# A fused cross-attention and fp4 feed-forward kernel on one core: a split first load of the gate weights, and a new written order for the opening

## What is computed

```python
# attention over channels C = 256, in G = 8 groups of 32; inp_q = layernorm(x), inp_k = inp_v = ctx
t = Wt @ ctx;  p = Wp @ q;  g = Wg @ ctx
att = sum over a group's channels and all columns of (p * g) * SCALE
a = groupnorm(Wz[group] @ (att * t)) * gamma + beta + ctx
x = x + a
# feed-forward on layernorm(x); both operands of each product are quantized to fp4 in blocks of 16
def fp4_quant_dequant(x):
    scale = max(max(abs(block)) / 6, 1e-12)
    return GRID[searchsorted(MID, abs(block / scale))] * sign * scale
gate = fp4(x2) @ fp4(w_gate).T;  y = fp4(x2) @ fp4(w_up).T
out = x + fp4(silu(gate) * y) @ fp4(w_down).T          # w_gate, w_up: 1408 x 512; w_down: 512 x 1408
```

## Time and profile before

| what | value |
|---|---|
| median of 3 runs | 1752.34 us (1751.98 to 1753.92) |
| the profiled execution | 1750.55 us, its span 1748.7 us |
| TensorE busy | 1682.2 us, 96% of the span |
| VectorE busy | 1518.2 us, 87% |
| ScalarE, GpSimd busy | 825.2 us (47%), 705.9 us (40%) |
| TensorE busy from 60.00 to 102.05 us | 29.33 us of 42.05 |
| start of the first `hidden` | 102.05 us |

### The profile page before, as it was taken

How to read it: one execution, slowest core, us unless ns; L and a number is a source line. 1 busy time by engine, 2 the same in 40 slices (tenths; PEclk the granted TensorE clock), 3 DMA queues, 4 the chain that set the end, 5 groups by cost and what they waited for, 6 DMA issues and landing times.

```text
span 1748.7 us, 27776 instructions
## 1 busy us (share of the span) xinstructions
PE 1682.2 (96%) x8712; PEld 919.9 (53%) x8712; DVE 1518.2 (87%) x2569; ACT 825.2 (47%) x1470; POOL 705.9 (40%) x879
## 2 busy tenths in 40 slices
PE   2789999999999999999999999999999999999997
PEld 1666555555555555555555555555555555555543
DVE  8987888889888988898888889888988898888885
ACT  3656444544445454444454444445444444455321
POOL 6865333334444333344433334444333344443210
PEclk9999999999999999999999999999999999999998
DMA  7123344343433343344433443433443434343322
GB/s 256 34 43 73 87 92 95 87 99 88 104 71 92 88 101 91 91 97 80 94 93 89 90 99 86 105 75 88 92 101 87 98 89 94 80 93 88 64 58 51
DMA packets 415094, 156.59 MB, mean 90 GB/s; under 512 B 386144, under 2 KB 387424, under 8 KB 415072
## 3 DMA queue, kind: packets, MB, share of 16 engines
q1 hardware_dynamic: 399296, 125.89, 33.7%
q10 hardware_dynamic: 15776, 30.41, 5.4%
HBM read 43.03 MB, written 16.78 MB: 34 GB/s over the span
## 4 chain that ended last, share of the span: by engine, by line
PE 92%; DVE 4%; DMA 1%; ACT 1%; issue 1%; SPq 0%; POOL 0%; DVEq 0%; ACTq 0%
PE pairs L561 51%; PE work L572 25%; PE work L511 4%; PE work L523 3%; PE ubank L538 2%; PE work L538 2%; PE pairs L601 1%; DMA hT_parts<-raw 1%; PE work L583 1%; DVE w_rinv L1191 0%; DVE work L1448 0%; PE pairs L511 0%; DMA raw<-in_L_ffn_w_gate 0%; DVE x_in L1209 0%; PE pairs L593 0%
## 5 line engine op out<-in xcount | busy, mean ns | idle before, releaser
L561 PE MATMUL pairs<-w_gate_hi,xT_parts 128*128 128x512 f16 (+1 forms) x1536 | 555.8, 362 | 1.8 <-DMA xT_parts<-raw 1.4
L561 PE MATMUL pairs<-w_up_hi,xT_parts 128*128 128x512 f16 (+1 forms) x1536 | 555.1, 362 | 0.0
L572 PE MATMUL work<-w_parts,hT_parts 128*128 128x512 f16 x2079 | 458.9, 379 | 1.0 <-DMA hT_parts<-raw 1.0
L572 PEld LDWEIGHTS work<-w_parts,hT_parts 128*128 128x128 f16 x2079 | 203.3, 99 | 236.3 <-issue 1.1
L561 PE MATMUL pairs<-w_up_lo,xT_parts 128*128 128x512 f16 (+1 forms) x768 | 277.7, 362 | 0.0
L561 PE MATMUL pairs<-w_gate_lo,xT_parts 128*128 128x512 f16 (+1 forms) x768 | 277.7, 362 | 0.0
L561 PEld LDWEIGHTS pairs<-w_gate_hi,xT_parts 128*128 128x128 f16 x1536 | 152.5, 99 | 163.6 <-issue 15.2
L561 PEld LDWEIGHTS pairs<-w_up_hi,xT_parts 128*128 128x128 f16 x1536 | 150.2, 98 | 146.6
L952 ACT ACTIVATE early<-pairs,w_unit 128x512 f32<-128x512 f32 (+1 forms) x192 | 124.8, 650 | 166.9 <-PE pairs L561 166.9
L861 ACT CAST raw<-hq 128x704 f16<-128x704 f32 x126 | 98.1, 779 | 180.4 <-DVE hq L1187 179.7
L1395 DVE SCALAR_TENSOR_TENSOR h<-pairs,w_unit,early 128x512 f32<-128x512 f32 (+1 forms) x192 | 135.0, 703 | 41.8 <-ACT early L952 36.5
(11 more groups left out here) (188 smaller groups left out, 2799.1 us busy)
## 6 DMA issues: line engine op xcount, KB each, us to landing
out<-raw SPq DMA_DIRECT2D x64, 256.0 KB, 2.1
c_in<-in_ctx ACTq DMA_DIRECT2D x29, 512.0 KB, 3.8
x_in<-in_x ACTq DMA_DIRECT2D x29, 512.0 KB, 5.2
raw<-in_L_ffn_w_down SPq DMA_DIRECT2D x2, 1408.0 KB, 8.7
raw<-in_L_ffn_w_gate SPq DMA_DIRECT2D x2, 1280.0 KB, 8.2
w_parts<-in_L_ffn_w_up SPq DMA_DIRECT2D x2, 1280.0 KB, 9.1
x_in<-in_x SPq DMA_DIRECT2D x3, 512.0 KB, 4.0
c_in<-in_ctx SPq DMA_DIRECT2D x3, 512.0 KB, 4.6
```

The source lines that it names most:

```text
L561: mm = pe.matmul(pairs[:, pair, n, 0:b - a], xT[s][part][:, k, :], w1[n][wpart][:, k, a:b], start=(k == 0 and part == 0 and wpart == 0), s ...
L572: mm = pe.matmul(obank[:, :], hT[part][:, k, :], w2[wpart][:, k, :], start=(k == 0 and part == 0 and wpart == 0), stop=(k == KH - 1 and pa ...
```

## The change

The first three of the 11 rows of 512 columns that each partition holds of the gate weights (`FIRST` = 3, 768 KB in all, enough for chunk 0's 1408 columns) are loaded by a transfer of their own, issued ahead of x, with a semaphore `raw_first`. What is left of the first half's large transfer (two rows, 512 KB) follows x. VectorE's `weight_max(0, 0)` waits for `raw_first` and stands first in its list. The written lists of the opening are in another order on all four compute engines; the loops and the end of the kernel are as they were.

```diff
+    FIRST = -(-H // D)
@@ load_raw(f)
+                    if f == 0:
+                        whole = whole[:, FIRST * D:]
+                    a = FIRST if f == 0 else n * (r + 1)
                     sp.dma_start(whole.rearrange("p (r k) -> p r k", k=D),
-                                 raw_dram[m][:, n * (r + 1):n * (r + 1) + r, :]).then_inc(raw_loaded[f], 16)
+                                 raw_dram[m][:, a:n * (r + 1) + r, :]).then_inc(raw_loaded[f], 16)
@@ SyncE
+            sp.dma_start(staged_half(0)[:, 0:FIRST * D].rearrange("p (r k) -> p r k", k=D),
+                         raw_dram[0][:, 0:FIRST, :]).then_inc(raw_first, 16)
             load_x(0)
@@ weight_max(m, c)
-                if c % 2 == 0:
+                if n == 0:
+                    dve.wait_ge(raw_first, 16)
+                elif n == 1:
+                    dve.wait_ge(raw_loaded[0], 32)
+                elif c % 2 == 0:
@@ VectorE's list
+            weight_max(0, 0)
             ln1_moments(0, 0)
...
             weight_rowmax(0)
+            weight_top(0)
             normalise1(0, 0)
+            weight_max(1, 0)
+            ctx_power(0)
             attention_lo()
-            weight_top(0)
@@ ScalarE's list
             weight_grain(0)
             ctx_fit(0)
             ctx_hi(0)
+            scale_all(0)
             weight_grain(1)
...
             weights_lo(9)
             weights_lo(10)
+            grain_x(0)
             weights_hi(11)
@@ GpSimd's list
             weight_y(1)
+            ctx_root(0)
             add_ctx(0, 1)
-            ctx_root(0)
```

## The result

| kernel | median of 17 runs | ratio | profiled execution |
|---|---|---|---|
| before | 1751.89 us (1750.43 to 1753.92) | 1 | 1750.55 us |
| changed | 1748.73 us (1746.71 to 1751.98) | 0.9982, 95% interval 0.9975 to 0.9989 | 1748.85 us, span 1747.0 |

The median falls by 3.2 us, to the 1748.7 that was forecast. So the gain is 2 to 3 us. Both intervals leave out 1, but 3.2 us are 0.18%, less than the 0.2% that the prediction took as what a measurement of this kernel can tell from no change.

A forecast was written before the change was run, and what follows sets the result against it. Other engines set the opening up to the first hidden, TensorE's own work all after. 4.0 us gained there less 0.4 for low clock gives 3.6: 1752.34 to 1748.7 us, range 1743.5 to 1754.5.

The forecast's parts named there:

- The sum: Opening: first hidden at 96.9 instead of 102.05, less 1.1 us owed, gives 4.0 us; less 0.4 for clock, 3.6.
- a charge for the clock: TensorE's eight turn_again products behind new idle time run at 1.2 GHz; up to 0.8 us, half taken, 0.4.
- The prediction's own sign for the last: TensorE's share from the first hidden to 155 us below 95% would show the gain being handed back.
- the same: Outcome class for the measured time: no change that a measurement can tell, within 0.2% or 3.5 us; chance 0.42.
- Rival D: Split load costs about 2 us latency again: chunk 2 at 14.6, gain 1.7 us, median 1750.6; chance 7%.
- The walk: New opening lists stepped through with old durations, port waits lasting whole instructions; starts hidden(0, 0, 0) at 96.9.
- TensorE's idle time from 78.6 to 82.3: Up sets: ScalarE's grain_x(0), ahead of weights_hi(11), waits for x_y(0) until 81.1, 3.5 us idle on ScalarE.
- the wait of 4.07 us: TensorE's idle time before 90.16 at top_of_rows(2), waiting for weight_rowmax(2); forecast gone, as it moves behind sets 15 to 18.
- TensorE's 2.8 us of idle there stay: Rest of the opening, after hidden(0, 0, 1): VectorE as far ahead of TensorE as before, so 2.8 us idle remain.
- A: Rival: reordering only moves work past work, nothing is left of the gain; 1750.5 to 1752 us; chance 22%.
- B: Rival: grain_x(0) ties up sets to the x chain, port losses delay x_y(0); 3 us slower, 1755.5; chance 12%.
- C: Rival: TensorE's idle times of 3.92 and 4.07 us both vanish with most low clock; 1744.5 us; chance 9%.

The follow-up runs named there:

- e1: Kernel before with only the split first load and weight_max(0, 0) ahead of the statistics of x; 1751.27 us, ratio 1.0000 to before.
- e6: Changed kernel with attention_lo() moved up on VectorE right behind normalise1(0, 0); 1749.27 us, ratio 0.9989 to the kernel before.
- e7: e4 with weight_rowmax(1) moved up behind sum_pg(0, 1), weight_top(1) ahead of weight_round(5), weight_unit(1) ahead of normalise2(0); 1752.01 us, ratio 1.0001 to before.
- e5: Kernel before with top_of_rows(2) moved behind turn_weights(18), and spread_top(2), weight_top(2) moved back with it; 1750.84 us, ratio 0.9997 to before.
- e9: e7 with grain_x(0) moved on ScalarE behind weights_lo(11) instead of ahead of weights_hi(11); 1750.83 us, ratio 0.9992 to the kernel before.
- e4: Changed kernel with sum_pg(1, 0), (1, 1) ahead of weight_round(11) and ln1_moments(2, 0) ahead of h_snap_back(0) on VectorE; 1748.03 us, ratio 0.9979 to before.
- e12: e7 plus earlier rounds, later grain_x(0), earlier x chain, and weight_round(6) moved up behind residual(1, 1); 1748.87 us, ratio 0.9986 to before.

## Why the prediction was right, point by point

**The time** came within 0.1 us of the median, and part of that is luck. The sum had 4.0 us at the first `hidden` and 3.6 after a charge for the clock. Measured are 2.7 there, 3.36 at `hidden(0, 0, 2)`, 1.16 at `output(0)` and 1.7 in the spans; the medians differ by 3.2 in one set of runs and 2.2 in another, and by about 1.5 at an equal clock. Up to the first `hidden` the direction held, by way of the x steps. The sum was too large by `spread_top(2)`, 0.3 us, which TensorE owes beside `turn_again(18)` and which the sum left out, by the start of `hidden(0, 0, 0)` at 97.97 and not 96.9, and by what was handed back behind it. The prediction's own sign for the last, a share of TensorE up to 155 us below that of before, did not show it: 54.07 of 57.03 us from the first `hidden` on, against 50.19 of 52.95, 95% both. By the prediction's measure of 0.2% the outcome is its "the same", to which it gave 0.42, a little less than to "faster" (0.46).

**The load**: `raw_first` landed by 5.45 (4.9 forecast), chunk 1 started at 8.56 (8.7), chunk 2 at 12.31 (12.7), `weight_y(1)` at 17.56 (18.1). Rival D is refuted: the split costs nothing, in a DMA share of 0.94 at 340 GB/s. The Trainium skill (DMA: Bandwidth & Descriptors, on the fixed cost of a transfer) has a fixed cost of about 2 us per transfer, for transfers that GpSimd issues. In this full queue of SyncE's transfers it does not show: chunk 2 starts 1.0 us earlier and not later. D's price was also read too high: in the kernel before the first bytes of x moved about 1.1 us after its issue, not 2, and ten transfers of 256 KB or less stood among the large ones, not seven. e1 adds that this head start alone gains nothing.

**The new waits**: 2.38 us before `weight_top(0)` (2.5 forecast). `normalise1(0, 0)` took 0.52 us and not 2.37, since GpSimd's instruction ended at 20.15, before 20.7. `ctx_power(0)` ended at 23.56 (24.0), `weight_grain(0)` started at 24.38 (24.7), `weight_q(0)` ended at 37.35 (38.2). The walk blamed `attention_lo` for the lateness of `weight_q(0)`; e6 shows that it is not the cause.

**The middle**: `normalise2(0)` at 72.42 (72.7), `x_y(0)` ended at 80.56 (81.1), `x_quant(0)` at 85.0 (84.3), `weight_round(6)` at 88.2 (87.9), `weight_q(6)` at 91.4 (90.5). On this chain the walk held within 1 us over 90 us, with every port wait counted as a whole one. Part of that is luck too: `weight_unit(1)` ended at 76.5 and not at 74.3, since `ctx_power(1)` ahead of it took 2.56 us at the port, and `x_y(0)` ended 0.5 us early all the same, so the steps between the two met fewer waits than the walk allowed.

**TensorE's idle time from 78.6 to 82.3** did not come as one piece. The first up set was turned at 80.06 and not at 77.7, since `weight_q(4)` waited for `scale_all(1)`, which follows `weight_unit(1)`, until 77.42. So ScalarE stood only 0.58 us in `grain_x(0)`. The late set hid the wait. e7 made the set early, and the wait came in full.

**The step that failed in its reason**: "`top_of_rows(2)` is no longer in front of sets 15 to 18 ... so the wait of 4.07 us is gone". The wait did go, but not for that: e5 moves the place alone and keeps 4.24 us of wait. The other cause, ScalarE's 4.85 us in `grain_x(0)`, stood in the trace, and the walk did not list it as one. It went because the x steps came earlier (`x_y(0)` ended at 80.56 instead of 89.05). What took away the other idle time, the 3.92 us before 74.20, no run isolates; e1 and e5 keep it, and e7 and e9 have 3.30 us at the same step.

**The steps that failed in size**: "TensorE's 2.8 us of idle there stay" missed 1.77 us behind 135, which e4 takes away. The 0.4 us charged for a low clock did not come in the profiled execution; the clock was a gain there, 0.6 us, and over all executions more of the gain went with it than the sum had. A new 2.45 us at `top_of_rows(1)` was not foreseen. The bounds "1 + 2.6 to 6.2" should read 1.0 to 6.2, which is 3.6 less and plus 2.6.

**The rivals**: A is out, since the first `hidden` came at 97.97 and not after 100.5, but its idea returned in e7 to e12, where each wait taken away came back elsewhere. B was one list entry away. C is out: both idle times vanished, but TensorE idled 2.06 us less and not 8, in many pieces, of which 2.45, 1.19 and 1.25 us lie between 60 and 98 us.

## What to carry to other kernels

Before pricing a wait, list everything that ends in the last microsecond before its end, on every engine that feeds it: a second cause keeps the wait alive when the first is moved, and one move alone on the chip shows it. In a written order near its optimum, bringing a step forward is only worth something if what it releases does not stand against a later step of the same chain; on a shared port the released GpSimd work of 2.6 us can hit the very chain that was to be helped. And follow a gain at the end of one stage to the next milestones, since it can be handed back there, as it was here behind the first `hidden` and, in e4, behind `output(0)`.

## What the runs showed of the hardware

- How long VectorE waits for GpSimd at the shared port does not go by the size of its instruction. In e7 four steps of 128x1 beside GpSimd's `weight_y` took 0.13 to 0.16 us each, and soon after them `ctx_power(1)` on 128x2 took 2.55 us, up to the end of the next `weight_y` at 73.73:

```profile
70.66 0.15 DVE L1452 TENSOR_SCALAR w_gain<-w_pow 128x1 f32<-128x1 f32 x1
...
71.21 2.55 DVE L1182 TENSOR_SCALAR c_norm<-c_norm 128x2 uint32<-128x2 uint32 x1
```

  The Trainium skill (SBUF — State Buffer, on the exclusive lock of the shared port pair) has the exclusion; the runs agree, in both directions (1.53 us for GpSimd in the changed kernel). The four steps on a single column did not wait.
- The idle time just before a stretch does not alone decide TensorE's clock. In the changed kernel it was 0.58 from 59 to 63 us and 1.00 from 63 to 67, and an idle time of 2.45 us before 67.03 did not bring it down: 1.00 from 67 to 80. In e6 it was 0.51 from 59 to 63 us and stayed low, 0.52 from 67 to 80, with an idle time of only 1.47 us before 66.55. In e6's profiled execution the low stretch came with a first `hidden` 1.8 us later.
